# Row maxima written by two transfers of 48 source partitions a row, in place of four of 24

## The chip, the cores and the metric

One core of one Trainium2 chip. The metric is the device time of one execution in microseconds (us). Engines: PE (TensorE, matmuls), DVE (VectorE), ACT (ScalarE), POOL (GpSimd) and SP (SyncE), which here issues nearly all transfers.

## The reference, cut to what matters

The input is 32 images of 56 x 56 x 24. A block of shifted-window attention with an MLP comes first, then a convolution block with a SiLU, then two pairs of a Fourier mixer and a quantised feed-forward part. The change lies in the window attention:

```python
shifted = jnp.roll(x, (-SHIFT, -SHIFT), axis=(1, 2))
win = _window_partition(shifted)              # 7 x 7 windows: L = 49
h = _layernorm(win, ln1_g, ln1_b)
q = (h @ wq).reshape(-1, L, NH, d)            # NH = 3 heads, d = 8
k = (h @ wk).reshape(-1, L, NH, d)
v = (h @ wv).reshape(-1, L, NH, d)
attn = jnp.einsum('nqhd,nkhd->nhqk', q, k) / jnp.sqrt(jnp.float32(d))
attn = attn.reshape(B, nW, NH, L, L) + mask[None, :, None]
attn = jax.nn.softmax(attn, axis=-1)
out = jnp.einsum('nhqk,nkhd->nqhd', attn, v)
```

## The kernel before

The 32 images go in 8 quads of 4 (q = 0 to 7; QI = 4). In a quad each image has 32 of the 128 partitions, 24 of them channels; partition 28 of the 32 holds a constant or, here, a bias. Every quad goes through window attention, MLP, convolution, and twice mixer and feed-forward. There is no scheduler: each engine's program is written out by hand, and semaphores order the engines.

Window attention takes a quad in 8 rows of 8 windows (t or u = 0 to 7), and a row in 4 steps of two windows (n = 4t + dw). It computes the scores twice. The first time (queries by keys) DVE takes the maximum over the keys (L977, into `mx`). PE turns the maxima with an identity, ACT copies them negated into `mxt` (L775): 48 partitions, which are 2 groups of images by 8 windows by 3 heads, each with 49 values for either of two images. SP then writes each as a row of 1176 values (24 x 49) onto partition 28 of its image in the masked queries `qm`, by transfers from SBUF to SBUF (L510, in `write_max_rows`). The second time (turned scores: keys by `qm`, whose partition 28 now subtracts the maximum) ACT takes the exponential (L741), and PE weighs the values with it.

In the profile `mxt`, `mx`, `qs` and `ks` lie in the tensor area_hz, `qm` and the exponentials in area_ty, and all of PE's matmuls stand at the helper's line L1131.

For row t, the order around the change is:
- PE's `max_turned` and ACT's L775 for row u are made at step dw = 1 of row u - 1; for row 0 that is ahead of the first step of the quad.
- SP waits for the copy (`max_kept`, L506) and for the masked queries (`q_masked`, L507), then issues the transfers of that row; each adds 16 to the semaphore `max_rows`.
- PE waits for all transfers of row t at the row's first step (L1235), behind the first scores of step n + 6 (AHEAD = 6). At step 0 of a quad it waits also for the first 6 maxima (`maxed`, L1239), for the turned scores go to the banks 2 and 3 that the odd ones among the first scores used.
- ACT, before it copies row u, waits for the transfers of row u - 2 (L774), since `mxt` has two buffers.

In quad 0, SP starts the loads of the transform tables (`load_transforms`, L490 to L495) once all rows of the maxima are written (L518), and behind them in the same queue it loads the first mixer table (L500, area_hz<-f_all), for which PE waits at the start of the mixer (L1472). In later quads only the mixer tables, the next input and the stores of the result (L456) are in SP's queue.

Of the kernel before, what the change touches and what calls it, by code (L numbers as in the profile page):

```python
# [23 lines left out]
QI = 4  # L24
NQ = B // QI
RW = 32
WS, SHIFT, NH, DH = 7, 3, 3, 8
L = WS * WS
NW = HW // WS
# [15 lines left out]
PADL = 64  # L45
# [147 lines left out]
def query_bank(u):  # L193
    return 6 if u else 5


def key_bank(u):
    return 7 if u else 4
# [16 lines left out]
def step_of(l, stage, j=0):  # L215

    return l * LAYER_STEPS + sum(ST_STEPS[:stage]) + j
# [47 lines left out]
def build_kernel(nc, x, keep, raw, g2, g4, out, nq=NQ):  # L265
    ctx = ExitStack()
    with ctx:
# [3 lines left out]
        def sem(name):  # L271
            return ctx.enter_context(nc.semaphore(name))
# [50 lines left out]
        def part(area, at, *shape):  # L323
            n = int(np.prod(shape))
            v = area[:, at:at + n]
            if len(shape) == 2:
                v = v.rearrange("p (a b) -> p a b", b=shape[1])
            if len(shape) == 3:
                v = v.rearrange("p (a b c) -> p a b c", b=shape[1], c=shape[2])
            return v, at + n  # L330
# [6 lines left out]
        mxt, at = part(area_h, at, 2, SIDE)  # L337
        assert at <= 2 * NTOK
        qm, at = part(area_t, 0, 3, NW, NH * L)
# [62 lines left out]
        max_turned, max_kept, max_rows = sem("max_turned"), sem("turned_max_kept"), sem("max_rows_written")  # L402
# [39 lines left out]
        def _(sp):  # L442
# [44 lines left out]
            def load_transforms():  # L487

                for r in (0, 64):
                    sp.dma_start(g2_sb[r:r + HW, :, HW:3 * HW], g2[0:HW, 0:HALF, :]).then_inc(tables_loaded, 16)  # L490
                    sp.dma_start(g2_sb[r:r + HW, :, 0:HW], g2[64:64 + HW, 0:HALF, 0:HW]).then_inc(tables_loaded, 16)
                sp.wait_ge(gaps_zeroed, 1)
                for r in (0, 64):
                    for g in range(2):
                        sp.dma_start(g4_sb[r + HALF * g:r + HALF * (g + 1), :, g, :], g4[r:r + HALF, :, :]  # L495
                                     ).then_inc(tables_loaded, 16)

            def load_table(q, l):

                sp.dma_start(f1s[0:121, :, :], f1_all[l].rearrange("p (s n) -> p s n", n=2 * HW)  # L500
                             ).then_inc(table_loaded, 16)

            def write_max_rows(q):

                for t in range(NW):
                    sp.wait_ge(max_kept, q * NW + t + 1)  # L506
                    sp.wait_ge(q_masked, q * NW + t + 1)  # L507
                    for j in range(QI):
                        g, jj = j // 2, j % 2
                        sp.dma_start(  # L510
                            qm[RW * j + 28:RW * j + 29, t % 3, :, :].rearrange("p w (h n) -> p (w h) n", n=L),
                            mxt[NW * NH * g:NW * NH * g + NW * NH, t % 2, PADL * jj:PADL * jj + L]
                        ).then_inc(max_rows, 16)

            def tables(q, between):

                if q == 0:
                    sp.wait_ge(max_rows, NW * 64)  # L518
                    load_transforms()
                sp.wait_ge(attended, q * NW + NW)  # L520
                sp.wait_ge(table_stored, 2 * CI // CHUNK * 16)
                load_table(q, 0)
                sp.wait_ge(reordered, q * NW + NW)
                between()
                sp.wait_ge(filled, q * FILLS + step_of(0, ST_F2))
                load_table(q, 1)
# [166 lines left out]
        def _(act):  # L693
# [40 lines left out]
            def window_attention(q):  # L734
                for n in range(-8, STEPS + 4):
                    t, dw = n // 4, n % 4
                    if 0 <= n < STEPS:
                        act.wait_ge(cross, q * STEPS + n + 1)
                        if n >= 2:
                            act.wait_ge(weighed, q * STEPS + n - 1)  # L740
                        act.activation(pt[0:SIDE, n % 2, :, :], ps[0:SIDE, 2:4, 0:6 * L], ACT.Exp  # L741
                                       ).then_inc(exped, 1)
                    if dw == 0 and 0 <= t - 1 < NW:
                        act.wait_ge(weighed, q * STEPS + 4 * t)
                        if t - 1 >= 2:
                            act.wait_ge(out_normed, q * NW + t - 2)
                        act.activation(osb[:, (t - 1) % 2, :], ps[:, 4, 0:TW], ACT.Copy
                                       ).then_inc(out_kept, 1)
                    if dw == 0 and t + 2 < NW:
                        u = t + 2  # L750
                        act.wait_ge(k_made, q * NW + u + 1)
                        if u >= 3:
                            act.wait_ge(cross, q * STEPS + 4 * u - 8)
                            act.wait_ge(k_masked, q * NW + u - 2)
                        act.activation(ks[:, u % 3, :, 0:L], ps[:, key_bank(u), 0:TW].rearrange("p (w n) -> p w n", n=L),
                                       ACT.Copy).then_inc(k_kept, 1)
                        act.wait_ge(q_made, q * NW + u + 1)
                        if u >= 2:
                            act.wait_ge(scored, q * STEPS + 4 * u - 4)
                            act.wait_ge(q_masked, q * NW + u - 1)  # L760
                        act.activation(qs[:, u % 2, :, 0:L], ps[:, query_bank(u), 0:TW].rearrange("p (w n) -> p w n", n=L),
                                       ACT.Copy).then_inc(q_kept, 1)
                    if dw == 1 and 0 <= t - 1 < NW:
                        act.wait_ge(sum_spread, q * NW + t)
                        act.activation(lns, ps[:, 5, 0:TW], ACT.Ln).then_inc(sum_logged, 1)
                        if t - 1 >= 1:
                            act.wait_ge(out_normed, q * NW + t - 1)
                        act.wait_ge(sum_logged, q * NW + t)
                        act.activation(rec, lns, ACT.Exp, scale=-1.0).then_inc(sum_inverted, 1)
                    if dw == 1 and 0 <= t + 1 < NW:  # L770
                        u = t + 1
                        act.wait_ge(max_turned, q * NW + u + 1)
                        if u >= 2:
                            act.wait_ge(max_rows, q * NW * 64 + 64 * (u - 1))  # L774
                        act.activation(mxt[0:2 * NW * NH, u % 2, :], ps[0:2 * NW * NH, 6, 0:SIDE], ACT.Copy,  # L775
                                       scale=-1.0).then_inc(max_kept, 1)
                    if dw == 2 and 0 <= t - 2 < NW:
                        square(q, LN_WIN2, t - 2)
                    if dw == 3 and 0 <= t - 2 < NW:
                        invert(q, LN_WIN2, t - 2)  # L780
                square(q, LN_WIN2, NW - 1)
                invert(q, LN_WIN2, NW - 1)
# [346 lines left out]
        def _(pe):  # L1129
# [67 lines left out]
            def window_attention(q):  # L1197

                def quadrants(bank, still, moving, w, dst):
                    for j in range(QI):  # L1200
                        g, jj = j // 2, j % 2
                        r = slice(RW * j, RW * j + RW)
                        ins = mm(ps[PADL * jj:PADL * jj + PADL, bank + g, dst:dst + NH * L],
                                 still[r, w, :], moving[r, w, :])
                    return ins
# [9 lines left out]
                for n in range(-8, STEPS + 4):  # L1215
                    t, dw = n // 4, n % 4
                    k = n + AHEAD
                    if 0 <= k < STEPS:

                        u = k // 4  # L1220
# [11 lines left out]
                    if 0 <= n < STEPS:  # L1232

                        if dw == 0:
                            pe.wait_ge(max_rows, q * NW * 64 + 64 * t + 64)  # L1235
                        if n >= 1:
                            pe.wait_ge(exped, q * STEPS + n)
                        else:
                            pe.wait_ge(maxed, q * STEPS + AHEAD)  # L1239
                        pe.sem_inc(passed_pe, 1)  # L1240
                        for i in range(2):
                            ins = quadrants(2, ks[:, t % 3], qm[:, t % 3], 2 * dw + i, NH * L * i)
                        ins.then_inc(cross, 1)
                    k = n - 1
                    if 0 <= k < STEPS:

                        u = k // 4
# [5 lines left out]
                        for i in range(2):  # L1253
                            w = 2 * (k % 4) + i
# [7 lines left out]
                    if dw == 0 and 1 <= t + 2 < NW:  # L1262

                        u = t + 2
# [17 lines left out]
                    if dw == 1 and 0 <= t + 1 < NW:  # L1282

                        u = t + 1
# [499 lines left out]
```

## Time and profile before

| what | value |
|---|---|
| time, 3 runs | median 3509.89 us (3506.67 to 3512.7) |
| the profiled execution | span 3515.2 us; no time of its own outside the span is given |
| PE busy | 3115.1 us, 89% of the span |
| DVE busy | 1704.2 us, 48% |
| ACT busy | 1625.4 us, 46% |
| mean granted clock of PE | 0.980 |
| waits of PE for the rows of maxima | 20.1 us in 18 waits |

Busy times are sums over one execution. The line of waits is what PE stood still for, by the transfer that released it. A group names what an instruction writes and reads (out<-in), its size and its count. SPq is SP's queue of transfers: the duration of such an entry is the time that SP needs to issue it, not the time in which the data moves.

### The profile page before, as it was taken

To read this page: it belongs to the slowest core of one execution; us is meant where nothing else is said; L and a number is where in the kernel's file an instruction comes from. 1 tells how busy PE (TensorE), PEld (TensorE's weight loads), DVE (VectorE), ACT (ScalarE), POOL (GpSimd) and SP (SyncE) were. 2 spreads that over 40 slices of the span, in tenths; PEclk is the share of its full clock that TensorE was granted. 3 is DMA by queue.
4 is the path that set the end of the run, shared out by engine and by line. 5 is a ranking of instruction groups with operands and counts; after the bars stand their busy time and mean duration, and the time that the engine had idled before them with its cause. 6 is when DMAs were issued, how large, how long until landed. Compare 5 with 4: busy or idle time off the path is not lost.

```text
span 3515.2 us, 110460 instructions
## 1 busy us (share of the span) xinstructions
PE 3115.1 (89%) x49194; PEld 1970.0 (56%) x49194; DVE 1704.2 (48%) x2740; ACT 1625.4 (46%) x2883; POOL 359.9 (10%) x574
## 2 busy tenths in 40 slices
PE   6968889888898888998989889998899988999888
PEld 3536646466465574554745647546465474564744
DVE  5424555355553545444454545635455354563544
ACT  3542354633546325554355443463544535445344
POOL 4510010000100001001000011000110001100011
PEclk9989999999999999999999999999999999999999
DMA  2322000110001100110001100011000210001100
GB/s 80 67 49 51 2 15 4 50 31 2 16 4 50 32 2 16 22 50 13 2 17 33 50 1 2 17 51 32 2 2 17 51 32 1 2 18 33 32 1 15
DMA packets 31252, 84.83 MB, mean 24 GB/s; under 512 B 24818, under 2 KB 25954, under 8 KB 26930
## 3 DMA queue, kind: packets, MB, share of 16 engines
q1 hardware_dynamic: 29506, 72.56, 8.7%
q8 instruction: 396, 6.49, 0.8%
q0 software_dynamic: 1280, 5.21, 0.5%
q14 instruction: 70, 0.57, 0.1%
HBM read 61.70 MB, written 14.84 MB: 22 GB/s over the span
## 4 chain that ended last, share of the span: by engine, by line
PE 72%; ACT 12%; DVE 5%; issue 5%; SPq 4%; DMA 3%; ACTq 0%; DVEq 0%
PE ps L1131 72%; ACT lv L719 2%; SPq L495 2%; ACT rs L724 2%; ACT area_ty L853 2%; DMA area_ty<-area_hz 1%; ACT sq L707 1%; SPq L510 1%; DMA area_hz<-f_all 1%; DVE xs L1102 1%; ACT area_ty L845 1%; ACT sq L705 1%; DVE area_ty L1098 1%; ACT area_ty L805 1%; ACT area_ty L811 1%
## 5 line engine op out<-in xcount | busy, mean ns | idle before, releaser
L1131 PE MATMUL ps<-area_hz 32*64 32x147 f32 (+2 forms) x7180 | 357.7, 285 | 84.7 <-DMA area_hz<-f_all 28.8
L1131 PE MATMUL ps<-area_ty,area_hz 113*64 113x49 f32 (+1 forms) x10240 | 393.5, 250 | 22.1 <-DMA area_ty<-area_hz 20.1
L829 ACT ACTIVATE area_hz<-ps 121x384 f32<-121x384 f32 (+2 forms) x256 | 129.6, 519 | 582.9 <-PE ps L1131 582.9
L1131 PE MATMUL ps<-sq,keep_sb 64*64 64x392 f32 (+1 forms) x1728 | 335.1, 531 | 71.0 <-ACT sq L707 44.0
L1131 PEld LDWEIGHTS ps<-area_hz 32*64 32x64 f32 (+2 forms) x7180 | 287.8, 154 | 191.2 <-issue 168.7
L1131 PEld LDWEIGHTS ps<-area_ty,area_hz 113*64 113x64 f32 (+1 forms) x10240 | 332.0, 135 | 104.1 <-issue 103.5
L1131 PE MATMUL ps<-area_ty,g_sb 56*112 56x192 f32 (+1 forms) x3712 | 311.8, 321 | 26.0 <-DVE area_ty L1074 19.7
L977 DVE TENSOR_REDUCE area_hz<-ps 113x12 f32<-113x588 f32 x256 | 196.4, 770 | 273.7 <-PE ps L1131 272.9
L944 DVE TENSOR_TENSOR area_ty<-ps,rs 128x392 f32<-128x392 f32 (+2 forms) x304 | 197.5, 650 | 260.0 <-ACT rs L724 259.9
L1131 PEld LDWEIGHTS ps<-area_ty,g_sb 56*112 56x112 f32 x3712 | 293.3, 173 | 44.7 <-issue 44.0
L1074 DVE COPY area_ty<-ps 120x896 f32<-120x896 f32 (+1 forms) x192 | 164.8, 858 | 262.8 <-PE ps L1131 262.8
L1131 PE MATMUL ps<-xs,keep_sb 64*64 64x448 f32 (+1 forms) x1184 | 219.8, 542 | 63.1 <-DVE xs L1102 48.0
L719 ACT ACTIVATE lv<-ps 128x448 f32<-128x448 f32 (+1 forms) x304 | 158.5, 522 | 253.0 <-PE ps L1131 253.0
L741 ACT ACTIVATE area_ty<-ps 113x588 f32<-113x588 f32 x256 | 168.8, 659 | 222.1 <-PE ps L1131 219.2
L829 ACT ACTIVATE area_ty<-ps 120x896 f32<-120x896 f32 (+1 forms) x192 | 140.2, 730 | 264.5 <-PE ps L1131 264.5
L1131 PEld LDWEIGHTS ps<-sq,keep_sb 64*64 64x64 f32 x1728 | 84.1, 133 | 297.0 <-ACT sq L707 135.5
L707 ACT ACTIVATE sq<-ps 128x448 f32<-128x448 f32 (+1 forms) x304 | 156.8, 535 | 177.9 <-PE ps L1131 176.2
L724 ACT ACTIVATE rs<-lv 128x448 f32<-128x448 f32 (+2 forms) x368 | 223.7, 608 | 32.7
L617 POOL CAST area_ty<-area_ty 128x1344 fp8e5<-128x1344 f16 x112 | 146.1, 1305 | 870.2 <-DVE area_ty L1109 870.2
L1131 PE MATMUL ps<-keep_sb,area_hz 112*58 112x56 f32 (+1 forms) x6144 | 196.8, 229 | 17.7 <-ACT area_hz L829 16.0
L1131 PEld LDWEIGHTS ps<-keep_sb,area_hz 112*58 112x58 f32 (+1 forms) x6144 | 193.9, 141 | 21.1 <-issue 20.8
L1085 DVE SCALAR_TENSOR_TENSOR xs<-ps,bn_bias,xs 128x448 f32<-128x448 f32 x112 | 76.6, 684 | 233.7 <-PE ps L1131 233.7
(123 smaller groups left out, 4306.2 us busy)
## 6 DMA issues: line engine op xcount, KB each, us to landing
area_hz<-f_all SPq DMA_DIRECT2D x16, 2541.0 KB
xw<-x_in SPq DMA_DIRECT2D x8, 1568.0 KB, 6.5
y_out<-xs SPq DMA_DIRECT2D x32, 252.0 KB
f_all<-piece POOLq DMA_DIRECT2D x16, 317.6 KB, 3.4
area_ty<-area_hz SPq DMA_DIRECT2D x256, 4.6 KB
area_hz<-raw_in SPq DMA_DIRECT2D x1, 2894.0 KB, 9.4
g_sb<-g_in SPq DMA_DIRECT2D x6, 355.2 KB
g_sb<-g_in SPq DMA_DIRECT2D x2, 710.5 KB
```

Source lines behind the costliest of these rows:

```text
L495: sp.dma_start(g4_sb[r + HALF * g:r + HALF * (g + 1), :, g, :], g4[r:r + HALF, :, :]).then_inc(tables_loaded, 16)
L617: gp.tensor_copy(hq8[:, i % 2, :, :], r16, saturate=False).then_inc(f_hid, 1)
L707: act.activation(sq[:, k % 2, 0:w], ps[:, center_bank(k), 0:w], ACT.Square).then_inc(squared, 1)
L719: act.activation(lv[:, k % 2, 0:w], ps[:, variance_bank(k), 0:w], ACT.Ln).then_inc(logged, 1)
L724: act.activation(rs[:, k % 2, 0:w], lv[:, k % 2, 0:w], ACT.Exp, scale=-0.5).then_inc(root, 1)
L741: act.activation(pt[0:SIDE, n % 2, :, :], ps[0:SIDE, 2:4, 0:6 * L], ACT.Exp).then_inc(exped, 1)
L829: act.activation(dst, src, ACT.Relu if st in (ST_H, ST_F2) else ACT.Copy).then_inc(sc_kept, 1)
L944: ve.tensor_tensor(o, a, b, ALU.mult, **kw).then_inc(normed, 1)
L977: ve.tensor_reduce(mx[0:SIDE, u % 2, :].rearrange("p (g c r) -> p g c r", g=2, c=4)[:, :, k % 4], ps[0:SIDE, score_bank(k):score_bank(k) + ...
L1074: ins = ve.tensor_copy(dst, src)
L1085: ve.scalar_tensor_tensor(xs[:, sl], ps[:, 7, 0:TT], bn_bias[:, l:l + 1], xs[:, sl], ALU.add, ALU.add).then_inc(ve_kept, 1)
L1131: return pe.matmul(o, a, b, start=start, stop=stop)
```

## The change

The loop over the four images of a quad becomes a loop over the two halves of `mxt`'s free dimension. One transfer reads all 48 partitions and writes partition 28 of two images, which lie 64 partitions apart, in place of two transfers of 24 partitions with one destination partition each. The counts of `max_rows` go from 64 to 32 a row, for PE, for ACT and for the wait ahead of the transform loads. Nothing else is changed, and the bytes are the same.

```diff
                 for t in range(NW):
                     sp.wait_ge(max_kept, q * NW + t + 1)
                     sp.wait_ge(q_masked, q * NW + t + 1)
-                    for j in range(QI):
-                        g, jj = j // 2, j % 2
+                    for jj in range(2):
+
                         sp.dma_start(
-                            qm[RW * j + 28:RW * j + 29, t % 3, :, :].rearrange("p w (h n) -> p (w h) n", n=L),
-                            mxt[NW * NH * g:NW * NH * g + NW * NH, t % 2, PADL * jj:PADL * jj + L]
+                            qm[RW * jj + 28:RW * jj + 28 + 65:64, t % 3, :, :].rearrange("p w (h n) -> p (w h) n", n=L),
+                            mxt[0:2 * NW * NH, t % 2, PADL * jj:PADL * jj + L]
                         ).then_inc(max_rows, 16)
...
-                    sp.wait_ge(max_rows, NW * 64)
+                    sp.wait_ge(max_rows, NW * 32)
                     load_transforms()
...
-                            act.wait_ge(max_rows, q * NW * 64 + 64 * (u - 1))
+                            act.wait_ge(max_rows, q * NW * 32 + 32 * (u - 1))
...
-                            pe.wait_ge(max_rows, q * NW * 64 + 64 * t + 64)
+                            pe.wait_ge(max_rows, q * NW * 32 + 32 * t + 32)
```

SP's queue in quad 0, between the set-up loads and the transform loads (- before, + with the change; a row names line, out<-in, the destination's shape and the count):

```order
 L481 DMA terms<-raw_in 1x48 x2
 L484 DMA w<-raw_in 32x32 x3
-L510 DMA area_ty<-area_hz 1x24x49 x32
+L510 DMA area_ty<-area_hz 2x24x49 x16
 L490 DMA g_sb<-g_in 56x29x112
 L491 DMA g_sb<-g_in 56x29x56
```

The 32 issues of the eight rows of quad 0 become 16, each with two destination partitions; what stands before and behind them is the same.

SP's queue in a later quad, between the stores of the quad before and the load of the first mixer table:

```order
 L456 DMA y_out<-xs 24x2688 x4
 L456 DMA y_out<-xs 24x448 x4
-L510 DMA area_ty<-area_hz 1x24x49 x32
+L510 DMA area_ty<-area_hz 2x24x49 x16
 L500 DMA area_hz<-f_all 121x5376
 L448 DMA xw<-x_in 128x3136
```

The same in all eight quads: the rows of the other engines are word for word those of before.

## Rows read from the trace of the kernel before

**Rows 1.** The page: busy times of the engines, and the chain that ended last.
```profile
PE 3115.1 (89%) x49194; PEld 1970.0 (56%) x49194; DVE 1704.2 (48%) x2740; ACT 1625.4 (46%) x2883; POOL 359.9 (10%) x574
...
PE 72%; ACT 12%; DVE 5%; issue 5%; SPq 4%; DMA 3%; ACTq 0%; DVEq 0%
```

**Rows 2.** Waits: engine line <- releaser: us in total, times, longest us.
```profile
PE ps L1131 <- DMA area_hz<-f_all: 28.8, 1, 28.8
PE ps L1131 <- DMA area_ty<-area_hz: 20.1, 18, 2.8
```

**Rows 3.** The chain, quad 1's start (start us, us, what); then L510's issues (ns).
```profile
515.37 0.27 ACT area_hz L775
515.63 0.02 issue
515.65 0.83 SPq L510
...
518.11 1.92 DMA area_ty<-area_hz
520.02 0.14 issue
...
531.61 77.44 PE ps L1131 x1628
...
L510 SPq DMA_DIRECT2D area_ty<-area_hz x256: 729/732/1818, 53.7 to 3182.8; - x128
```

**Rows 4.** Timelines of DVE and PE, first rows of quads 1 and 6 (start, us).
```profile
518.83 0.77 DVE L977 TENSOR_REDUCE area_hz<-ps 113x12 f32<-113x588 f32 x1
520.16 0.73 PE L1131 MATMUL ps<-area_ty,area_hz 32*64 32x147 f32 x16 [1.51 <-DMA area_ty<-area_hz]
...
2663.21 0.77 DVE L977 TENSOR_REDUCE area_hz<-ps 113x12 f32<-113x588 f32 x1
2665.87 1.26 PE L1131 MATMUL ps<-area_ty,area_hz 32*64 32x147 f32 x16 [2.85 <-DMA area_ty<-area_hz]
```

**Rows 5.** Timeline of PE: later waits, two of quad 0, three of quads 2 to 6.
```profile
70.91 1.57 PE L1131 MATMUL ps<-area_ty,area_hz 32*64 32x147 f32 x40 [1.02 <-DMA area_ty<-area_hz]
...
97.71 1.57 PE L1131 MATMUL ps<-area_ty,area_hz 32*64 32x147 f32 x40 [0.58 <-DMA area_ty<-area_hz]
...
973.74 1.45 PE L1131 MATMUL ps<-area_ty,area_hz 32*64 32x147 f32 x36 [0.41 <-DMA area_ty<-area_hz]
...
2246.16 1.57 PE L1131 MATMUL ps<-area_ty,area_hz 32*64 32x147 f32 x40 [0.89 <-DMA area_ty<-area_hz]
...
2756.16 3.16 PE L1131 MATMUL ps<-area_ty,area_hz 32*64 32x147 f32 x80 [0.55 <-DMA area_ty<-area_hz]
```

**Rows 6.** The chain, end of quad 0's attention to the start of its mixer.
```profile
146.72 3.10 DMA area_ty<-area_hz
149.82 0.01 issue
149.84 0.36 SPq L490
...
208.16 20.97 SPq L495
...
229.23 41.41 DMA area_hz<-f_all
270.65 0.25 issue
```

**Rows 7.** Issues of two other lines: ns min/median/max, first and last start.
```profile
L500 SPq DMA_DIRECT2D area_hz<-f_all x16: 292/302/20852, 229.2 to 3289.1; - x16
...
L456 SPq DMA_DIRECT2D y_out<-xs x64: 302/370/1643, 502.3 to 3513.2; - x64
```

**Rows 8.** Transfers, 515 to 521 us, then 186.4 to 208: packets, MB, share.
```profile
q1 hardware_dynamic: 144, 0.02, 2.3%
...
q1 hardware_dynamic: 1625, 0.36, 7.5%
```

**Rows 9.** Windows behind the first rows of quads 1 and 6; clock third from last.
```profile
520.80:524.20 3.40, 3.40 (x24) 1.33 (x24) 0.77 (x2) 1.62 (x3) 0.00 (x0) 0.50 0.00 0
...
2664.40:2671.20 6.80, 5.33 (x48) 2.91 (x52) 1.56 (x3) 1.67 (x3) 0.00 (x0) 0.50 0.00 0
```

## The prediction

> **What bounds the kernel now.** I read the page first: PE is busy 3115.1 of 3515.2 us, and the chain that ended last runs 72% of the span over PE [rows 1]. The reader is to see that only what keeps PE waiting, or what the load of a stage waits for, can move the time. The waits on the transfers at issue come next: PE waited 18 times, 20.1 us in all, for the rows of negated maxima (area_ty<-area_hz), and once 28.8 us for the first mixer table (area_hz<-f_all) [rows 2]. These 18 waits are what the change can reach. The chain around one of them shows how it is made up [rows 3]: ScalarE's copy of the turned maxima ends at 515.64, SP issues four transfers, the fourth at 518.11, it lands 1.92 us later, and PE starts its turned scores 0.14 us after that. Each issue takes 0.73 us with a gap of 0.05. From the first issue to the last landing that is 518.11 + 1.92 - 515.65 = 4.38 us. Between the rows PE runs without a break: 77.44 us in one piece from 531.61 [rows 3], so PE time that is won in a row stays won.
>
> **The change, part by part.**
>
> *Issues.* 128 of 256 go: two a row of windows in place of four, over 64 rows. On SP itself this is worth nothing, since SP idles; it counts only as the time to the last landing. What one of the new issues takes (two destination partitions, 48 source partitions) no row shows. The nearest is the old issue of the same line, 0.73 us [rows 3]; I take that. Below stands the issue of a store from 24 partitions, 0.30 us at least (median 0.37), and of a table load of 121 partitions, 0.29 [rows 7]; above, an issue whose cost goes by its packets, twice 0.73 = 1.46 us.
>
> *Spread over the rings.* The four transfers of 24 pieces each left 144 packets in their window: 96 pieces of 196 bytes, and 48 more, which I read as one closing packet for each DMA engine in use, so 12 engines a transfer. The transfer of 29 partitions left 1625 packets for its 1624 pieces in 21.6 us [rows 8]: one engine, 13.3 ns a packet. 12 is the largest number up to 16 that divides 24, for 29 it is 1, and for the change's 2 destination partitions against 48 sources it would be 2: 24 pieces an engine in place of 2, so 22 x 13.3 ns = 0.3 us later at the last landing. The bounds are 3 pieces on each of 16 engines (nothing) and 48 on one (0.6 us). Behind this: the Trainium skill, "DMA: Bandwidth & Descriptors", section "Why a DMA increments its semaphore by 16 and not by 1", states that the engines used are the largest number up to 16 that divides the slowest dimension of both sides. The trace agrees, with 12 and 1. Its section "Rules for kernel authors" speaks against this change, for it warns that an outermost dimension under 16 confines the DMA to that many engines. By that rule alone the last landing comes 0.3 us later; by the old spread the sum below would differ by that 0.3 us at one place.
>
> *Landing.* New: 0.73 + 0.05 for the first issue, 1.92 from the second's start to landing, 0.3 for the fuller rings: 3.00 us, against 4.38. The rows land 1.38 us earlier. With issues of 0.29 it is 0.34 + 1.48 + 0.3 = 2.12, so 2.26 us earlier; with 1.46 it is 1.51 + 2.65 + 0.3 = 4.46, so 0.08 us later.
>
> *The eight first rows, one a quad.* Their waits are 13.1 us of the 20.1, but little of it is free. The turned scores of step 0 go to banks 2 and 3, which VectorE's sixth maximum must have read (the wait on maxed for AHEAD). In quad 1 that reduce ends at 519.60 [rows 4], so PE can start at 519.74 at the earliest, not at 520.16: 0.42 us of 1.51. The other quads of ordinary length give the same, 0.34 to 0.41. In quad 6 the reduce ends at 2663.98 and PE starts at 2665.87 [rows 4]: at most 1.75, but there the wait outlasts its usual length by 1.4 us, of which part may be something else; I take 1.0. Quads 1 to 7: 0.42 + 5 x 0.35 + 1.0 = 3.2 us. Here VectorE's reduce is late next.
>
> *The seven later waits in quads 1 to 7* are 0.41 to 0.89 us each [rows 5], together 20.1 - 13.1 - 2.2 (quad 0's) = 4.8. All are shorter than 1.38, so all go: 4.8 us. PE has no other wait there: it ran its whole queue up to each.
>
> *Quad 0.* Its end is set by SP, not by PE. The last row's transfers land at 149.82, the transform loads start then, run to 229.1 in one queue, and the table load behind them lands at 270.65, for which PE waits 28.8 us [rows 6]. So the quad ends earlier by PE's gains ahead of the last row, 0.41 in the first row and 1.02 and 0.58 later [rows 5], and by the last landing itself, 1.38 (its own PE wait of 0.63 is under the cover): 3.4 us.
>
> *Edits at nothing.* The wait of ScalarE's copy for the transfers of two rows back, and the counts that are halved, change no order: PE, VectorE, ScalarE and GpSimd issue what they did. The bytes are the same.
>
> **Sum:** 3.2 + 4.8 + 3.4 = 11.4 us. The profiled execution has a span of 3515.2 us, 5.3 above the median of the runs, 3509.9; its own time outside the span isn't given. The profile would go to 3503.8, the median to **3498.5 us**. About 0.2% (7 us) is what a measurement of this kernel can tell from no change.
>
> **The rivals.**
>
> 1. *An issue costs by its pieces.* Then two new issues take what four old ones took, the rows land 0.08 us later, and nothing moves: 3510. For it: the old issue, with just 24 pieces, takes 0.73 us where stores take 0.37 [rows 7]. Against it: the first transform load, 1624 pieces, was issued in 0.36 us [rows 6].
>
> 2. *Other waits close behind.* PE starts a row earlier and then waits for an exponential or a maximum, so half of the 8.0 us in quads 1 to 7 is given back: 3502.5, and with the waits of another execution, which need not be those of this one, down to 6 us of gain, 3504. Against it: PE's unbroken 77 us.
>
> 3. *Slower: SP is held by two full rings.* If a ring takes no more than some packets ahead of the engine, the 24 pieces of the first transfer hold SP in its issue. The longest issue of this line is 1.82 us, and the loads that go over one engine hold SP 21 us each [rows 3, 6]. Where an issue lasts longer than x with (x + 0.05) + (x + 1.19) + 0.3 = 4.38, x = 1.42, it is a loss. At 1.82 the rows land 0.8 us late: eight first rows 6.4, ten waits there are now 8.0, some eight more rows that now just make it 5.6, quad 0 0.8: 20.8 us, 3531. Against it: 24 packets take 0.3 us, less than one issue.
>
> 4. *The clock comes along.* After the first rows of quads 1 and 6 PE's granted clock was 0.50, the lower of its two levels (1.2 GHz), for 3.4 and 6.8 us; PE had idled 1.5 and 2.9 us ahead [rows 9]. In quad 3 it was the same for 3.4 us. PE was busy 3.4 + 3.4 + 5.3 = 12.1 us of these, which at 2.4 GHz would be half: if the shorter waits spare all three, 6.0 us more, 3492.5. Against it: the wait ahead shrinks by 0.4 us only, and four quads with the same wait kept the full clock.
>
> **How the numbers follow.** The forecast 0.58, rival 1 0.13, rival 2 0.12, rival 3 0.07, rival 4 0.10. The range 3492 to 3507 takes in rival 4, rival 2, and most of the forecast's own spread: the issue at 0.29 gives quad 0 0.9 and quad 6 0.75 more, 3497, the median of a few runs is uncertain by some 3 us, and it leaves out rivals 1 and 3. Faster: the forecast and rival 4, less what noise takes, 0.65, and a third of rival 2, 0.04: 0.69. Slower 0.07. The rest, 0.24, is within 0.2%.
>
> **What would show it.** In the profile of the changed kernel: 128 issues of the line at 0.73 us; from the first issue to the landing in the chain 3.0 us; the window of one row with 96 pieces and 4 closing packets; PE's waits for area_ty<-area_hz gone, and the first rows' waits put down to VectorE's reduce, 1.1 us each; the table of quad 0 landing near 267.3. Wrong I would be if the issues took 1.4 us or more, if the waits stayed near 20 us, or if new waits of PE in attention made up for them.

## The result, and the profile after

The changed kernel takes 3490.76 us (median of 4 executions, 3483.66 to 3492.41) against 3508.28 for the kernel before beside it: ratio 0.9937, 95% interval 0.9915 to 0.996. Run again as a kernel of its own it took 3490.77 beside 3512.48, ratio 0.9937 (0.9922 to 0.9953). That is 17.5 us in the first group and 21.7 in the second, which has far more executions of the kernel before (19 against 4); 11.4 were forecast. The median lies 1.2 us below the range.

The profiled execution took 3489.36 us, with a span of 3487.6. That of before had a span of 3515.2, which is high among the executions of before, so the two profiles differ by more than the medians.

The new issues of the transfers (ns min/median/max), against [rows 3]:

```profile
L510 SPq DMA_DIRECT2D area_ty<-area_hz x128: 492/502/627, 54.0 to 3151.5; - x128
```

Two at 0.50 us stand where four at 0.73 stood. The waits of PE, against [rows 2] (engine line <- releaser: us in total, times, longest):

```profile
PE ps L1131 <- issue: 44.0, 64, 1.4
PE ps L1131 <- DMA area_hz<-f_all: 28.5, 1, 28.5
...
PE ps L1131 <- DVE area_hz L977: 7.9, 17, 0.5
```

The 18 waits for area_ty<-area_hz are gone, all of them. In the page's terms the transfers' share of the chain fell from 3% to 1%:

```profile
PE 73%; ACT 12%; DVE 6%; issue 5%; SPq 3%; DMA 1%; ACTq 0%; DVEq 0%
```

The first row of quad 1, against [rows 4] (timelines of PE, then of DVE):

```profile
511.82 0.73 PE L1131 MATMUL ps<-area_hz 32*64 32x147 f32 x16 [0.47 <-DVE area_hz L977]
513.61 0.61 PE L1131 MATMUL ps<-area_ty,area_hz 32*64 32x147 f32 x12 [1.06 <-issue]
...
512.73 0.77 DVE L977 TENSOR_REDUCE area_hz<-ps 113x12 f32<-113x588 f32 x1
```

PE still idles, 1.06 us in place of 1.51, and starts 0.11 us after VectorE's sixth maximum ends at 513.50. So the reduce is what is late next; the profile calls the wait "issue" and not DVE, since it names a releaser only where the times fit. The landing of the last row of quad 0, and the load behind it, against [rows 6] (the chain: start us, us, what):

```profile
142.10 0.50 SPq L510
142.60 0.04 issue
142.64 2.35 DMA area_ty<-area_hz
...
145.00 0.34 SPq L490
...
225.50 41.57 DMA area_hz<-f_all
267.07 0.25 issue
```

From the first issue to what waits for the landing it is 145.00 - 142.10 = 2.9 us here, 5.4 in the same row before (149.82 - 144.38). That row isn't a usual one: its landings took 3.10 us before and 2.35 here from the last issue on. The packets of the other 63 rows tell what is usual: from a row's first issue to the end of its last packet the median is 3.98 us before (3.84 to 5.95) and 2.02 after (2.01 to 2.33). So the rows are written 1.96 us earlier, and the delays of up to 2 us that single rows had are gone as well. The transfers of one row, 509 to 514 us, against the first row of [rows 8]:

```profile
q1 hardware_dynamic: 100, 0.02, 2.0%
```

100 packets are 96 pieces and 4 closing ones: two engines for each of the two transfers. And the clock in the first row of quad 1: it read 0.50 in [rows 9] from 5.4 us after the start of ScalarE's copy (515.37) on. Here the copy starts at 509.27, and the same stretch reads 1.00 (third number from the end):

```profile
514.67:518.07 3.40, 3.40 (x84) 2.40 (x82) 2.34 (x4) 2.06 (x4) 0.00 (x0) 1.00 0.02 5
```

ScalarE's copy of the maxima (L775) is a clock for the rows of windows. The table gives the time from its start in one row to its start in the next, in us, worked out from ScalarE's timeline, as the smallest to the largest of the eight quads in the profiled executions.

| kernel | row 1 to 2 | row 2 to 3 | row 3 to 4 | rows 1 to 8, all quads |
|---|---|---|---|---|
| before | 9.87 to 13.77 | 11.61 to 12.57 | 12.13 to 12.85 | 711.9 |
| changed | 9.49 to 11.55 | 11.33 to 11.41 | 12.14 | 692.2 |
| changed, again | 9.49 to 13.08 | 11.33 to 12.19 | 12.13 to 12.14 | 698.9 |

From row 4 on both kernels take 13.66 us a row and 12.13 for the last, save some rows in quad 0 (14.40 before, 14.02 in the changed kernel run again). In that second profile of the changed kernel 3.4 us of the 6.7 by which its rows are longer lie in quad 0.

### The profile page after: what moved, and what is told of

Read it like the earlier page. It is cut to its first block, busy times and chain, and to the rows that moved or that the text cites. A ratio compares the mean times of both kernels' runs of the same rounds, so it can differ in the third digit from the quotient of the medians.

```text
span 3487.6 us, 110332 instructions
## 1 busy us (share of the span) xinstructions
PE 3103.2 (89%) x49194; PEld 1969.6 (56%) x49194; DVE 1705.0 (49%) x2740; ACT 1626.4 (47%) x2883; POOL 359.9 (10%) x574
## 4 chain that ended last, share of the span: by engine, by line
PE 73%; ACT 12%; DVE 6%; issue 5%; SPq 3%; DMA 1%; ACTq 0%; DVEq 0%
PE ps L1131 73%; ACT lv L719 2%; ACT area_ty L853 2%; SPq L495 2%; ACT rs L724 2%; DMA area_hz<-f_all 1%; DVE xs L1102 1%; ACT sq L707 1%; ACT area_ty L845 1%; ACT area_ty L805 1%; ACT sq L705 1%; ACT area_ty L811 1%; DVE area_hz L994 1%; DVE area_ty L1098 1%; DVE area_hz L977 1%
## 5 line engine op out<-in xcount | busy, mean ns | idle before, releaser
L1131 PE MATMUL ps<-area_hz 32*64 32x147 f32 (+2 forms) x7180 | 357.0, 284 | 84.6 <-DMA area_hz<-f_all 28.5
L1131 PE MATMUL ps<-area_ty,area_hz 113*64 113x49 f32 (+1 forms) x10240 | 391.7, 249 | 11.3 <-issue 8.5
```

Source lines behind the costliest of these rows:

```text
L1131: return pe.matmul(o, a, b, start=start, stop=stop)
```

## The experiments

The kernels below ran beside 11 to 23 executions of the kernel before each, which has a median between 3511.4 and 3514.9 in these groups.

**The changed kernel again.**

> The changed kernel once more, for more executions of it beside the kernel before. If its gain is what the waits of PE account for (11.6 us less waiting in attention, 2 us at quad 0's transform loads), the medians differ by 12 to 16 us. If the clock belongs to it (low-clock stretches behind the shorter waits gone), by 16 to 22 us.

Measured: 3490.77 us, 21.7 below the kernel before. That is the case in which the clock belongs to the gain. Over all executions (70 of the kernel before, 10 of the changed) the mean granted clock is 0.9805 and 0.9844. With two levels, the lower half of the upper, the time at the lower is twice the missing share of the span: 137 and 109 us. Among the 70 executions of the kernel before alone, one with 1 us more at the lower clock takes 0.35 us longer. 28 us less would so be some 10 us of the 22. This is a correlation, from clocks given to three digits: a longer wait can bring both the lower clock and the longer time. Nor does all of this low-clock time cost anything. The longest stretch of it in the profile of before lies in the wait of 28.8 us for the mixer table, where PE has 4.1 us of work:

```profile
244.30:275.00 30.70, 4.10 (x40) 4.13 (x42) 0.52 (x1) 0.92 (x1) 0.00 (x0) 0.50 0.60 141
```

**Spare transfers ahead.** Two of the old form, onto a scratch tile, ahead of the real ones in each row:

```diff
+            def spare(q, t):
...
+                for i in range(2):
+                    p = 2 * t + i
+                    sp.dma_start(scr[p:p + 1, :, :], keep_sb[0:24, 49 * i:49 * i + 49]).then_inc(scr_done, 16)
...
+                    spare(q, t)
                     for jj in range(2):
                         sp.dma_start(
```

> The changed kernel with two spare transfers of the old form (24 source partitions, one destination partition of a scratch tile) ahead of the two real ones in every row: the last landing moves from about 2.4 to about 3.9 us behind the first issue, the number of transfers is four again. Theory 1, the moment of landing decides: nearly the time before comes back, 3502 to 3508 us. Rival, it is the number of packets and transfers on the engines: 3508 here, and 3500 or more in the kernel with the spare ones behind.

Measured: 3502.8 us, ratio 0.9974 (0.9961 to 0.9988): 12 us slower than the changed kernel. That is within the range of theory 1. The waits are back by half, as they should be with a landing between the two:

```profile
PE ps L1143 <- DMA area_ty<-area_hz: 10.0, 11, 1.2
```

10.0 us here, 20.1 in [rows 2], none in the changed kernel.

**The same spare transfers behind.** The same call after the two real transfers in place of ahead of them.

> The same two spare transfers, issued behind the real ones: the same number and packets, but the landing stays early. Theory 1: no change against the changed kernel, 3488 to 3493 us (quad 0's transform loads start at most 1 us later). Rival: as slow as with the spare ones ahead, 3500 us or more.

Measured: 3493.85 us, ratio 0.9943 (0.993 to 0.9956). Just above the range given, 3 us from the changed kernel and 9 from the one with the spare ones ahead. The two kernels move the same packets; when the rows land makes the difference. Theory 1 holds, and the rival on packets falls as the cause of the gain; the 3 us are within what the medians of a few executions can be.

**Idle matmuls in the first wait, kernel before.**

```diff
+                        if n == 0:
+                            keep_busy(5, 3)
                         if dw == 0:
                             pe.wait_ge(max_rows, q * NW * 64 + 64 * t + 64)
```

> The kernel before with three idle matmuls (0.40 us each) in the wait of each quad's first row, which is 1.45 us: no wait ends earlier. Theory 2, the lower clock behind these waits is part of the gain: the stretches at 0.50 behind the first rows go, 3502 to 3505 us. Rival, the clock has no part: 3508 us as the kernel before, or up to 2 us more.

Measured: 3507.07 us, ratio 0.9981 (0.9969 to 0.9992), 5.4 below: between the two cases. My duration was wrong by half: each call is two passes, so three calls took 2.5 us:

```profile
514.37 2.52 PE L1131 MATMUL ps<-keep_sb 128*128 128x448 f32 x6
516.82 0.73 PE L1131 MATMUL ps<-area_ty,area_hz 32*64 32x147 f32 x16
```

That made PE late: rows 1 to 2 took 10.8 to 11.4 us in every quad, with no low-clock stretch, and rows 1 to 8 of all quads 712.0, as in the profile of before. The kernel is faster all the same, and its mean clock in all executions is 0.9828 against 0.9805. So the clock seems to have given it something, though one profile of each shows no gain over the attention's rows: the first steps of quads 1 to 7 sum to 76.1 us against 79.1, and what follows up to row 8 to 545.8 against 542.1.

**One idle matmul, kernel before.** The same with `keep_busy(5, 1)`.

> The kernel before with one idle matmul (two passes, 0.8 us) in the wait of each quad's first row, where three took 2.4 us and made PE late by some 0.7. No wait ends earlier and none later. Theory 2: the first row's step to the second is 9.9 us in the quads without a code fetch, with no low-clock stretch behind it, and the time is 5 to 9 us below the kernel before. Rival: 3511 us, no difference.

Measured: 3511.46 beside 3514.91, ratio 0.999 (0.9976 to 1.0004). That is less than theory 2 said, and the interval doesn't shut out the rival. In the profile rows 1 to 2 take 9.88 to 9.96 us in five quads, as expected. But quad 2 held 3.4 us at the lower clock there in spite of the matmul, and the step behind it took up to 12.8 (and 14.8 in quad 0), where the kernel before had 12.6 at most. One profile of each can't tell whether PE waited later for what it won early.

**The joined transfers in the first row of each quad only.**

```diff
+def joined(t):
+    return t == 0
...
+                    if joined(t):
+                        for jj in range(2):
...
+                        continue
                     for j in range(QI):
...
```

> The joined transfers in the first row of each quad only; the other seven rows keep four. PE starts the turned scores 0.4 us earlier in each quad: 3 us. If the low-clock stretches behind these waits belong to the gain (theory 2), 3 to 6 us more: 6 to 9 us below the kernel before. If the clock has no part: 3 us below.

Measured: 3507.24 us, ratio 0.9984 (0.9969 to 0.9998), 5.7 below. Between the two cases, and near the 6 of the one with the clock: 2.7 us of it are the earlier start (0.38 us in each of seven quads), and the interval of some 5 us either way takes in both. No first row of quads 1 to 7 held the lower clock in its profile.

**In the other seven rows only.** As above with `return t >= 1`.

> The joined transfers in rows 2 to 8 of each quad, the first keeps four. The later waits (7 us), some 0.26 us in each second row that the profile doesn't list as a wait (2 us) and 2 us at quad 0's transform loads: 10 to 12 us below the kernel before; the rest of the whole gain (22 us) is then the first rows'. Rival, the gain is all in the first rows: under 5 us.

Measured: 3502.45 us, ratio 0.9973 (0.9961 to 0.9985), 10.4 below. As expected. The two halves add up to 16 us, the whole is 22; each has an interval of some 5 us either way, so that says little. In this kernel the first rows still took 11.5 to 11.7 us in four quads of eight, 9.9 to 10.0 in three, and 14.1 in quad 0. One of quads 1 to 7 (quad 5) held 3.4 us at the lower clock in it.

**Idle matmuls in the changed kernel.** `keep_busy(5, 2)` at the same place.

> The changed kernel with two idle matmuls in each quad's first wait, which is now 1.1 us. Theory 2 says that the shorter wait no longer brings the lower clock, so there is nothing left to win: within 3 us of the changed kernel. Rival, the clock still falls there in some executions: 4 us or more below it.

Measured: 3492.99 us beside 3490.8, no gain. Rows 1 to 2 take 10.06 us in all quads, 0.57 more than the 9.49 without them, since the two calls outlast the wait. What spread there was in this step (up to 13 us) is gone, and no time is won with it. Nor did the clock rise: its mean over the six executions is 0.9823, against 0.9844 without the idle matmuls.

**The price of an issue.** Spare transfers in SP's idle time, each waited for before the next:

```diff
+sp.dma_start(scr[0:1, 0:24, :], keep_sb[0:24, 0:49]).then_inc(scr_done, 16)
+n[0] += 16
+sp.wait_ge(scr_done, n[0])
...
```

> The changed kernel with ten spare transfers of different shapes, three times, one after the other, each waited for, in SP's idle time of quad 0. If the issue costs by the engines used (2 engines 0.50 us, 12 engines 0.73: 23 ns an engine above 0.46): 16 rows 0.82, 8 rows 0.64, 23 rows (one engine) 0.48, 12 rows 0.73. If by the pieces: 8 rows under 0.5, 23 rows 0.72, 12 rows 0.5. If the landing goes by the pieces an engine has: 23 rows on one engine land 0.3 us later than 24 on 12.

Measured (issue, ns min/median/max), in this order: 24 partitions onto one; 48 onto two; 16, 12, 8 and 23 onto one; 24 onto two; 24 onto 24; 48 onto 48; 48 onto four.

```profile
L533 SPq DMA_DIRECT2D scr<-keep_sb x3: 764/767/848, 299.5 to 339.5; - x3
L536 SPq DMA_DIRECT2D scr<-keep_sb x3: 555/557/572, 301.5 to 341.4; - x3
L539 SPq DMA_DIRECT2D scr<-keep_sb x3: 548/548/585, 303.4 to 343.3; - x3
L542 SPq DMA_DIRECT2D scr<-keep_sb x3: 749/750/778, 305.9 to 345.4; - x3
L545 SPq DMA_DIRECT2D scr<-keep_sb x3: 636/636/637, 307.8 to 347.2; - x3
L548 SPq DMA_DIRECT2D scr<-keep_sb x3: 578/594/604, 311.2 to 348.9; - x3
L551 SPq DMA_DIRECT2D scr<-keep_sb x3: 557/559/563, 313.0 to 350.8; - x3
L554 SPq DMA_DIRECT2D scr<-keep_sb x3: 766/771/773, 314.7 to 352.4; - x3
L557 SPq DMA_DIRECT2D scr<-keep_sb x3: 540/540/540, 316.6 to 354.3; - x3
L560 SPq DMA_DIRECT2D scr<-keep_sb x3: 570/578/578, 319.8 to 356.1; - x3
```

Twelve pieces cost what 24 do (0.75 and 0.77 us), 48 pieces over 16 engines 0.54, and 24 onto 24 partitions what 24 onto one do: neither the pieces nor the shape set the price. The closing packets in the trace (the packets of each transfer less its pieces) confirm the engines that the common divisor gives: 12, 2, 16, 12, 8, 1, 2, 12, 16 and 4, in the order above. By the engines used the issue is 0.59 for 1, 0.56 for 2, 0.58 for 4, 0.64 for 8, 0.76 for 12, and 0.54 for 16. So it goes by the engines, but not in a line: 16 are the cheapest, where I had expected 0.82. The Trainium skill, "DMA: Bandwidth & Descriptors", section "Why a DMA increments its semaphore by 16 and not by 1", says that the issuing sequencer itself posts the increments of the engines that are not used. 16 engines leave none; that would fit their low price, but not that two engines are nearly as cheap, and no run here shows the mechanism.

From one issue to the next, which is the issue and the landing, the last round took:

```profile
339.51 0.76 SPq L533 DMA_DIRECT2D scr<-keep_sb  x1
341.45 0.56 SPq L536 DMA_DIRECT2D scr<-keep_sb  x1
343.29 0.55 SPq L539 DMA_DIRECT2D scr<-keep_sb  x1
...
348.89 0.60 SPq L548 DMA_DIRECT2D scr<-keep_sb  x1
350.76 0.56 SPq L551 DMA_DIRECT2D scr<-keep_sb  x1
352.44 0.77 SPq L554 DMA_DIRECT2D scr<-keep_sb  x1
```

1.94 us for 24 pieces over twelve engines, 1.84 for 48 over two, 1.68 for 24 over two. Twelve more pieces an engine cost 0.16 us, 13 ns each: the price of [rows 8]. But 23 pieces on one engine took 1.87 us, which is 1.27 after the issue, against 1.18 for 24 pieces over twelve engines: 0.1 us later and not the 0.3 expected. Counted from the start of the issue, the transfer over two engines lands sooner than the one over twelve with half its pieces.

**Split transform loads.** The prediction's rows show loads of 29 partitions at 21 us each; 28 has the divisor 14.

```diff
-                        sp.dma_start(g4_sb[r + HALF * g:r + HALF * (g + 1), :, g, :], g4[r:r + HALF, :, :]
-                                     ).then_inc(tables_loaded, 16)
+                        for a, b in ((0, HALF - 1), (HALF - 1, HALF)):
+                            sp.dma_start(g4_sb[r + HALF * g + a:r + HALF * g + b, :, g, :], g4[r + a:r + b, :, :]
+                                         ).then_inc(tables_loaded, 16)
...
-                pe.wait_ge(tables_loaded, 16 * 8)
+                pe.wait_ge(tables_loaded, 16 * 12)
```

> The changed kernel with each transform load of 29 partitions split into 28 and 1: 28 rows go over 14 engines instead of all over one (21 us each). The four take some 1.5 us each, the first mixer table is asked for at 172 us in place of 225 and lands ahead of PE, so the wait of 28.5 us in quad 0 goes: 28 to 33 us below the changed kernel, 3458 to 3463 us. If instead the loads are bound by their pieces in all, whatever the engines, nothing changes: 3491 us.

Measured: 3469.3 us, ratio 0.9873 (0.9852 to 0.9894) to the kernel before, 21.5 below the changed kernel: less than the 28 to 33 expected. SP's queue and PE at the mixer's second stage:

```profile
158.81 14.87 SPq L496 DMA_DIRECT2D g_sb<-g_in  x8
182.89 0.33 SPq L501 DMA_DIRECT2D area_hz<-f_all  x1
...
248.97 10.34 PE L1132 MATMUL ps<-area_hz 57*120 57x112 f32 x192 [0.70 <-DVE area_hz L1073]
```

The eight loads take SP 15 us in place of some 71, and PE's wait of 28.5 us is gone. Yet PE starts this stage 267.32 - 248.97 = 18.4 us earlier, not 28. The wait had covered PE's own delays in quad 0, which now count, and these differ between executions: in this one PE reached the mixer 9 us later than in the changed kernel's profile (238.82 against 229.37).

**Both, with idle matmuls.** `keep_busy(5, 2)`, then `keep_busy(5, 1)`, on top of the split loads:

> The same with the two idle matmuls in each quad's first wait. By theory 2 the shorter waits bring the lower clock seldom, so within 3 us of the kernel with split loads; if the lower clock still follows them often, 4 us or more below it.

Measured: 3471.76 us, ratio 0.9889 (0.9866 to 0.9912), within 3 us of the kernel with split loads.

> The changed kernel with split transform loads and one idle matmul (0.8 us) in each quad's first wait, which stays 1.1 us long. The lower clock rarely follows this wait, so 0 to 3 us below the kernel with split loads, 3466 to 3470 us. If the lower clock still follows it in most executions: 5 us or more below.

Measured: 3473.19 us, ratio 0.9879 (0.9855 to 0.9902). That is 3 us above the range. Neither is faster than the split loads alone, which stay the best of these kernels.

## Why the prediction was wrong

The direction and the path were right: the 20.1 us of waits went, all 18 of them, and nothing waits for these transfers now. The size was 11.4 where some 22 were measured, and the range ended at 3492. Some 15 of the 22 come from the waits, for which the sum had 11.4: 2.3 us of the difference are waits that the profile doesn't list, and 1.0 lies in the first rows. The rest goes with the clock, which the sum had at nothing.

- *Issues.* I took 0.73 us, that of the nearest row; it is 0.50. The term was the right one and mis-sized. It counts twice, for the 1.92 us from an issue's start to its landing hold an issue too. The bound below, taken from other lines at 0.29, held.
- *Spread.* Two engines a transfer: right. Said were 0.3 us for the fuller rings; from the end of the last issue to the last packet the median went from 0.78 to 0.98 us, 0.2 more.
- *Landing.* Forecast 1.38 us earlier, measured 1.96 in the usual row. That is 0.46 more by the issues and 0.1 by the spread. In the last row of quad 0 it was 2.5 (5.4 to 2.9), for this row's own delay, 1.2 us in the profile of before, is a part of that. This error cost the sum little: the waits of the later rows were all under 1.38 us, and in the first rows VectorE sets the bound.
- *First rows.* The bound by VectorE's sixth maximum was right to 0.03 us: the shortest step of rows 1 to 2 went from 9.87 to 9.49, 0.38 us, where 0.35 was said. But the longer ones of before, 11.3 to 13.8, I had read as this wait alone. Of quads 1 to 7, two (1 and 3) held 3.4 us at the lower clock in this step, quad 6 held 6.8, and two (2 and 4) a gap of 1.2 to 1.3 us that the profile puts down to issue. These seven gained 11.5 us in this step in the profiles (79.1 to 67.7), not 3.2: the waits for the rows of maxima give 4.2 of it (quad 6 alone 1.8, where I took 1.0), the end of the stretches at the lower clock 5.7 (PE's busy time in quads 1, 3 and 6 fell by 1.6, 1.6 and 2.4), and the gaps put down to issue 1.4.
- *Later waits.* Said 4.8 us in quads 1 to 7. Rows 2 to 3 also went from 11.62 to 11.37 where the profile of before showed no wait at all: PE's matmuls are modelled to end just when the next begin, so at least 0.25 us a quad was hidden. Between the copies of rows 2 and 8, quads 1 to 7 gained 5.7 us (542.1 to 536.4), where the listed waits make 3.4 and the hidden ones so 2.3; the other 1.4 of the 4.8 lie behind row 8.
- *Quad 0.* Said 3.4, and the table landing near 267.3. It landed at 267.07, 3.6 us earlier, or 3.8 with the 0.26 us by which the changed kernel's first row came later. PE's gains ahead (2.6) and the landing (2.5) were both larger than said; the transform loads gave 1.1 us back, 80.4 us in place of 79.3.
- *Rival 4, the clock.* This is the step that failed. I gave it 0.10 and put it at nothing in the sum, for the waits shrink by only 0.4 us. The granted clock of all executions rose from 0.9805 to 0.9844, and the time at the lower level fell by some 28 us. In the two profiles the waits give some 15 us: 4.2 in the first rows of quads 1 to 7, 5.7 between rows 2 and 8, 1.4 behind row 8, and 3.6 in quad 0. That leaves some 7 of the 22, and the correlation says some 10. Part of it lies where rival 4 has it. It priced the stretches of quads 1, 3 and 6 at 6.0 us, and they gave 5.7. The other profiles bear that out: with four transfers in the first row and no idle matmuls, 4 of 14 first rows of quads 1 to 7 held the lower clock (the kernel before and "other seven rows only"); with the joined transfers and nothing ahead of them, none of 42 (the changed kernel twice, and the runs with spare transfers behind, first rows only, priced shapes, and split loads). With the spare transfers ahead it was none of seven. So a wait that is only 0.4 us shorter was enough, which I had held to be too little; the runs don't show why.

The mean clock of each kernel over all its executions, and its gain against the kernel before in the same group (the changed kernel's from the second group):

| kernel | executions | gain, us | mean clock |
|---|---|---|---|
| before | 70 | | 0.9805 |
| changed | 10 | 21.7 | 0.9844 |
| spare transfers ahead | 7 | 9.7 | 0.9809 |
| spare transfers behind | 6 | 18.6 | 0.9830 |
| before, three idle matmuls | 12 | 5.4 | 0.9828 |
| before, one | 12 | 3.5 | 0.9822 |
| first rows only | 12 | 5.7 | 0.9814 |
| other seven rows only | 12 | 10.4 | 0.9802 |
| changed, two idle matmuls | 6 | 19.9 | 0.9823 |

Two rows tell the terms apart. The other seven rows alone leave the clock where it was and gain 10.4 us, which are waits. Three idle matmuls leave the attention's rows as long in all (712.0 us), raise the clock by 0.0023 (16 us less at the lower level), and gain 5.4, where 0.35 us for each microsecond would be 5.6.

*Rival 1* (issue by the pieces) is refuted by the priced shapes, *rival 3* by the issues of at most 0.63 us. *Rival 2* (other waits close behind) is not seen in the changed kernel. Where only the first row is joined, the later rows wait a little longer, but for the same transfers (8.0 us in the profile, against 7.0 before).

What stays open is where the rest of the clock's part arises. Filling the first waits of the kernel before gave 5.4 and 3.5 us, the second within its uncertainty, and in the first of these the attention's rows were no shorter in all. So it can't all be the stretch right behind the first waits, as I had put rival 4. Filling them in the changed kernel went with a lower mean clock in six executions, which nothing here explains. That the clock of the changed kernel is higher is measured; why it is, in stages which the change doesn't touch, isn't.

## What to carry to other kernels

Fewer and larger transfers helped here not by their bytes, but since a chain of issues on one queue stood between a result and the engine that waits for it: count issues up to the last landing, and ask what PE waits for once that is gone. Before shaping a transfer, look at the common divisor of both outer dimensions: here it decided the engines used, and with them the issue's price and, for 29 partitions, a load that held SP for 21 us and that 28 + 1 turns into 4. A wait on one profile is a sample; with a kernel whose executions spread by 10 us or more, compare the granted clocks of many executions before a difference is given to the waits alone.

## What the runs showed of the hardware that I had not expected

The issue of a transfer from SBUF to SBUF costs 0.54 us over 16 engines, 0.56 over 2, 0.64 over 8 and 0.76 over 12, there with 12 pieces as with 24. A transfer of 48 pieces over two engines is issued and landed in 1.84 us, one of 24 pieces over twelve in 1.94. And a long wait for a load (28.5 us in quad 0) hides PE's own delays, which differed by 9 us between two executions, so that taking it away gave 18.4 us there.
